# Second layer's attention in a two-layer kernel: three programs made one, and a quarter of its row maxima taken by way of ScalarE

## What is computed

```python
ct   = h @ [Wd_q | Wd_kv] + bias                 # 64 + 64 columns
q    = ct_q @ Wu_q + rope(ct_q @ Wq_r)           # 16 heads x 8
k    = ct_kv @ Wu_k + rope(h @ Wk_r)
v    = ct_kv @ Wu_v + bu_v
att  = softmax(q k^T / 12)                       # per batch and head, 1024 x 1024, no mask
x    = x + gate * ((att @ v) @ Wo + Wo_b)
```

## Time and profile before

| | us |
|---|---|
| median of three runs | 2776.39 (2762.96 to 2778.91) |
| the profiled execution | 2770.23 |
| its span | 2768.4 |
| TensorE's mean granted clock | 0.874 |
| busy: PE, DVE, ACT, POOL | 2131.2, 1554.8, 1210.0, 457.9 |

### The profile page before, as it was taken

How to read it: one execution, slowest core, us unless ns; L and a number is a source line. 1 busy time by engine, 2 the same in 40 slices (tenths; PEclk the granted TensorE clock), 3 DMA queues, 4 the chain that set the end, 5 groups by cost and what they waited for, 6 DMA issues and landing times. The chain is left out here.

```text
span 2768.4 us, 34114 instructions
## 1 busy us (share of the span) xinstructions
PE 2131.2 (77%) x11611; PEld 733.2 (26%) x11612; DVE 1554.8 (56%) x3124; ACT 1210.0 (44%) x1445; POOL 457.9 (17%) x548
## 2 busy tenths in 40 slices
PE   4346599999999999579768168888888867299964
PEld 2112133333333333323234011111111113233421
DVE  2865666665665663133433399999999923411101
ACT  2312144444444445222211047778778762155521
POOL 0000345454454542100022200000000000000000
PEclk8758599999999999689865569999999986599987
DMA  2000000000000000000011312112112010200000
GB/s 88 0 0 0 1 5 14 10 18 10 10 18 10 18 10 18 9 13 0 0 52 63 72 16 32 24 27 33 29 21 33 5 48 1 69 1 0 0 0 30
DMA packets 65751, 56.01 MB, mean 20 GB/s; under 512 B 37010, under 2 KB 49379, under 8 KB 65460
## 3 DMA queue, kind: packets, MB, share of 16 engines
q1 hardware_dynamic: 61188, 51.66, 8.3%
q10 hardware_dynamic: 4128, 2.43, 0.3%
q0 software_dynamic: 288, 0.00, 0.0%
HBM read 39.51 MB, written 13.89 MB: 19 GB/s over the span
## 5 line engine op out<-in xcount | busy, mean ns | idle before, releaser
L1370 DVE TENSOR_REDUCE h_m_half<-h_ps_max 128x1 f32<-128x512 f32 x1024 | 635.0, 684 | 35.3 <-PE h_ps_max L1277 31.2
L1353 ACT ACTIVATE h_P<-h_ps_st 128x1024 f32<-128x1024 f32 x512 | 495.2, 1022 | 110.4 <-PE h_ps_st L1296 109.6
L800 ACT ACTIVATE l_P<-l_ps_st 128x1024 f32<-128x1024 f32 (+3 forms) x384 | 307.0, 810 | 336.9 <-PE l_ps_st L707 335.5
L1277 PE MATMUL h_ps_max<-h_K,h_Q 48*128 48x512 bf16 x1024 | 209.0, 405 | 161.6 <-DVE h_m_half L1370 117.6
L707 PE MATMUL l_ps_st<-l_Q,l_K 64*128 64x512 f32 (+3 forms) x1536 | 329.1, 509 | 0.0
L884 DVE CUSTOM_DVE_ANT_0 l_masked<-l_ps_t,l_mask 128x384 bf16<-128x384 f32 (+3 forms) x512 | 230.3, 488 | 111.1 <-PE l_ps_t L665 110.6
L1306 PE MATMUL h_ps_o<-h_P,h_V 128*9 128x512 f32 x2048 | 268.9, 597 | 0.9 <-ACT h_P L1353 0.5
L887 DVE TENSOR_REDUCE l_m_half<-l_ps_t 128x1 f32<-128x512 f32 x256 | 164.9, 686 | 104.5 <-PE l_ps_t L665 102.6
L1695 PE MATMUL f_ps_h<-hT,f_W 128*128 x264 | 133.0, 651 | 74.5 <-issue 74.5
L1744 DVE TENSOR_TENSOR f_part<-f_biased,f_ps_w 128x512 f32<-128x512 f32 x33 | 22.7, 688 | 298.1 <-ACT f_biased L1722 298.1
L1277 PEld LDWEIGHTS h_ps_max<-h_K,h_Q 48*128 48x128 bf16 x1024 | 49.8, 93 | 494.5 <-DVE h_m_half L1370 437.4
(11 more groups left out here) (239 smaller groups left out, 2489.1 us busy)
## 6 DMA issues: line engine op xcount, KB each, us to landing
l_inv<-inverse_sums SPq DMA_DIRECT2D x64, 128.0 KB, 2.7
h_Q<-q_parts SPq DMA_DIRECT2D x192, 32.0 KB
h_K<-k_parts SPq DMA_DIRECT2D x192, 32.0 KB
f_W<-in_W SPq DMA_DIRECT2D x16, 256.0 KB
q_parts<-p_parts SPq DMA_DIRECT2D x4, 768.0 KB, 3.5
k_parts<-p_parts SPq DMA_DIRECT2D x4, 768.0 KB, 3.7
v_rows<-p_v_staged SPq DMA_DIRECT2D x4, 576.0 KB, 4.9
h_V<-v_rows SPq DMA_DIRECT2D x16, 144.0 KB
```

Of the source, the lines that this page charges most:

```text
L800: act.activation(P[e % PR][:, :, 0:w], ps_st[item(n, i, p) % 2][:, :, 0:w], ACT.Exp, scale=0.125).then_inc(consumed, 1)
L1277: pe.matmul(ps_max[:, (t + a) % NB, :], Q[n % NBUF][rows, p, qt * 128:(qt + 1) * 128], K[n % NBUF][rows, p, lo:lo + CH], start=True, stop= ...
L1353: act.activation(P[e % PR][:, :, :], ps_st[item(n, i, p) % 2][:, :, :], ACT.Exp, scale=1.0 / 12.0)\
L1370: dve.tensor_reduce(m_half[:, half, 2 * p + a, qt:qt + 1], ps_max[:, t % NB, :], AX.X, ALU.max, negate=True)\
```

## The change

Everything named here is the second layer's attention. Its three programs become one, `head_attention`. Its weights are loaded by 15 DMAs on ACT's queue in a small program of their own, `head_weights`, ahead of the first layer's experts. The eight products of batch 0 stand at the head of the program; those of batches 1 to 3 are put into the score loop by the table `AT`, one behind the last pair of a step, as are the output projections of batches 0 to 2. Each takes one of the two `ps_st` slots and an ACT instruction that empties it. Turning and splitting is a function `mix`, run by DVE for batch 0 and by POOL for the others. V stays on the chip. Outputs are kept in seven tiles `o`; SP sends the sums through DRAM, DVE inverts them (`invert`), POOL scales (`norm`) and adds (`join`). Loading a group takes 12 DMAs. The last group's chain of sums, scaling and projection stands at the end.

Of the 32 pairs of a group the eight in `FOLDED` (u = 4, 5, 12, 13, 20, 21, 28, 29) are no longer reduced from PSUM. ACT copies their four tiles to bf16 in `copied`, and DVE folds these by halves, 1024 to 512 to 256 elements wide, with three maxima of two operands and a last reduce, `LATER` = 5 pairs behind. So per group 64 reduces become 48, with 16 copies and four folds of four instructions.

PE's order in the score loop of group 0, first before (steps 2 and 3) and then after (the same steps). `h_ps_max` is a pair of maxima, `h_ps_st` scores or a product, `h_ps_o` values.

```diff
...
-def merge_heads(nc, S, A, l):
...
-def project_heads(nc, S, A):
...
-def head_scores(nc, S, A):
...
+def head_weights(nc, ctx, S, A):
+    def sb(name, shape):
+        return ctx.enter_context(nc.sbuf_tensor("h_" + name, shape, F32))
+    W = S.head = State()
+    W.Wd, W.bd, W.Wu, W.Wk, W.Wkv = sb("Wd", [D, 2, 64]), sb("bd", [128, 1]), sb("Wu", [64, 3, D]), sb("Wk", [D, 2, D]), sb("Wkv", [128, 2, D])
+    W.Wo, W.bv, W.cos, W.sin = sb("Wo", [128, NG, D]), sb("bv", [128, NG]), sb("cos", [128, T]), sb("sin", [128, T])
+    W.loaded = semaphore(nc, ctx, "h_weights_loaded")
+    W.count = 15
+    with nc.Block() as block:
         @block.scalar
         def _(act):
...
+            for to, x in ((W.Wd[:, 0, :], "Wd_q"), (W.Wd[:, 1, :], "Wd_kv"), (W.bd[0:64, :], "bd_q"), (W.bd[64:128, :], "bd_kv"),
+                          (W.Wu[:, 0, :], "Wq_r1"), (W.Wu[:, 1, :], "Wq_r1s"), (W.Wu[:, 2, :], "Wu_q"), (W.Wk[:, 0, :], "Wk_r1"),
+                          (W.Wk[:, 1, :], "Wk_r1s"), (W.Wkv[64:128, 0, :], "Wu_k"), (W.Wkv[64:128, 1, :], "Wu_v"), (W.bv[:, :], "bvG"),
+                          (W.cos[:, :], "cos1"), (W.sin[:, :], "sin1")):
+                act.dma_start(to, A[x]).then_inc(W.loaded, 16)
+            act.dma_start(W.Wo[:, :, :], A["WoG1"].rearrange("p (g d) -> p g d", g=NG)).then_inc(W.loaded, 16)
...
+    LEAD, TURN_AT, INVERT_AT = 6, 14, 8
+    NB, PR, NBUF, NOB, NLOAD, MIX = 3, 4, 4, 7, 12, 16
+    FOLDED = [u for u in range(NPAIR) if u // 4 % 2 and (u // 2) % 2 == 0]
+    LATER = 5
+    PROJECT = ("ct", "ka", "kb", "ku", "qa", "qb", "qu", "v")
+    AT = {}
+    for b in range(1, B):
+        for k, x in enumerate(PROJECT):
+            AT[(b - 1) * NG + k // 4, 2 + 3 * (k % 4)] = (x, b)
+    for b in range(B - 1):
+        for c in range(2):
+            AT[(b + 1) * NG + 2, 4 + 6 * c] = ("out", b, c)
...
+    order = [(x, 0) for x in PROJECT] + [("turn", 0)]
+    for n in range(NGR):
+        for i in range(NI):
+            if i == TURN_AT and n + 1 < NGR:
+                order.append(("turn", n + 1))
+            order += [("s", n, i, p) for p in range(2)]
+            if (n, i) in AT:
+                order.append(AT[n, i])
+    order += [("out", B - 1, c) for c in range(2)]
+    item = {x: k for k, x in enumerate(order)}
...
+        V = [sb(f"V{i}", [128, KT, H, M]) for i in range(2)]
         P = [sb(f"P{i}", [128, 2, CH]) for i in range(PR)]
...
+        o = [sb(f"o{i}", [128, T]) for i in range(NOB)]
+        inv = [sb(f"inv{i}", [128, T]) for i in range(2)]
+        flat = [sb(f"flat{i}", [128, HG * T // 128]) for i in range(2)]
+        moved = sb("moved", [D, T])
...
+        copied = [sb(f"copied{i}", [128, 2, 2, CH], BF16) for i in range(2)]
+        fold = [sb(f"fold{w}", [128, 2, w], BF16) for w in (512, 256, 128)]
...
+        def mix(eng, b, u, done, base):
+            a, t, w = a_[u], b_[u], u_[u]
+            at = base + (1 - u) * (MIX // 2)
+            eng.wait_ge(consumed, item[("qu", "ku")[u], b] + 1)
+            eng.tensor_tensor(a[:, :], a[:, :], cos[:, :], ALU.mult).then_inc(done, 1)
+            eng.tensor_tensor(t[:, :], t[:, :], sin[:, :], ALU.mult).then_inc(done, 1)
+            eng.wait_ge(done, at + 1)
+            eng.tensor_tensor(a[:, :], a[:, :], w[:, :], ALU.add).then_inc(done, 1)
+            eng.wait_ge(done, at + 3)
+            eng.tensor_tensor(a[:, :], a[:, :], t[:, :], ALU.add).then_inc(done, 1)
+            if b:
+                eng.wait_ge(parts_stored, 32 * b)
+            eng.wait_ge(done, at + 4)
+            eng.tensor_copy(parts[u][:, 0, :], a[:, :]).then_inc(done, 1)
+            eng.wait_ge(done, at + 5)
+            eng.tensor_tensor(a[:, :], a[:, :], parts[u][:, 0, :], ALU.subtract).then_inc(done, 1)
+            eng.wait_ge(done, at + 6)
+            eng.tensor_copy(parts[u][:, 1, :], a[:, :]).then_inc(done, 1)
+            eng.wait_ge(done, at + 7)
+            eng.tensor_tensor(parts[u][:, 2, :], a[:, :], parts[u][:, 1, :], ALU.subtract).then_inc(done, 1)
...
+        def load_part(eng, n, u):
+            src, to = (q1, k1)[u][n // NG], (Q, K)[u][n % NBUF]
+            for a in range(2):
+                lo, row = 64 * a, (n % NG) * 32 + 16 * a
+                rows = src[:, row:row + 16, :].rearrange("n (r p) t -> n r (p t)", p=2)
+                for count in (3, 2, 1):
+                    part = rows[0:count] if u else rows[3 - count].unsqueeze(0).broadcast_to([count, 8, 2 * T])
+                    eng.dma_start(to[lo:lo + 8 * count, :, :].rearrange("x p t -> x (p t)"), part).then_inc(loads[n % NBUF], 16)
+                    lo += 8 * count
...
+            def spread_sums(n):
+                sp.wait_ge(o_kept, 2 * n + 2)
+                sp.dma_start(sums1[n], o[n % NOB][8:128:32, :]).then_inc(sums_stored, 16)
+                sp.wait_ge(sums_stored, 16 * (n + 1))
+                if n >= 2:
+                    sp.wait_ge(inv_stored, 16 * (n - 1))
+                sp.dma_start(flat[n % 2][:, :], sums1[n].rearrange("j (x t) -> (j x) t", x=32)).then_inc(flat_loaded, 16)
+                sp.wait_ge(inverted, n + 1)
+                sp.dma_start(inv1[n].rearrange("j (x t) -> (j x) t", x=32), flat[n % 2][:, :]).then_inc(inv_stored, 16)
+                sp.wait_ge(inv_stored, 16 * (n + 1))
+                if n >= 2:
+                    sp.wait_ge(normed, 2 * (n - 1))
                 for j in range(HG):
...
+                    sp.dma_start(inv[n % 2][32 * j:32 * j + 32, :], inv1[n, j].partition_broadcast(32)).then_inc(inv_loaded, 16)
...
+            keep_parts(0, 1)
+            keep_parts(0, 0)
+            sp.wait_ge(ones_set, 2 * NBUF + 2)
+            sp.wait_ge(parts_stored, 32)
+            load_part(sp, 0, 0)
+            load(1)
             place_maxima(0)
             for n in range(NGR):
...
+                if n:
+                    spread_sums(n - 1)
+                if n % NG == 1 and n // NG + 1 < B:
+                    keep_parts(n // NG + 1, 1)
+                if n % NG == 2 and n // NG + 1 < B:
+                    keep_parts(n // NG + 1, 0)
+                if n + 2 < NGR:
+                    load(n + 2)
                 if n + 1 < NGR:
                     place_maxima(n + 1)
...
+            spread_sums(NGR - 1)
...
+            def free_slot(x):
+                if x >= 2:
+                    pe.wait_ge(consumed, x - 1)
+                return ps_st[x % 2]
...
+                elif kind == "out":
+                    pe.wait_ge(normed, 2 * NG * (b + 1))
+                    c = key[2]
+                    for g in range(NG):
+                        last = pe.matmul(to[:, 0:CH], Wo[:, g, :], o[(b * NG + g) % NOB][:, c * CH:(c + 1) * CH],
+                                         start=(g == 0), stop=(g == NG - 1))
...
-                if t + 2 > NB:
-                    pe.wait_ge(reduced, t + 2 - NB)
+                for x in (t - NB, t + 1 - NB):
+                    if x >= 0 and kept_by_copy(x):
+                        pe.wait_ge(max_copied, tiles_before(x, True) + 1)
+                    elif x >= 0:
+                        pe.wait_ge(reduced, tiles_before(x, False) + 1)
...
                             values(n if i else n - 1, (i - 1) % NI)
+                    if (n, i) in AT:
+                        product(AT[n, i])
             values(NGR - 1, NI - 1)
+            for c in range(2):
+                product(("out", B - 1, c))
...
+            def copy_maxima(n, u):
+                if n >= NGR or u not in FOLDED:
+                    return
+                k = n * len(FOLDED) // 2 + FOLDED.index(u) // 2
+                if k >= 2:
+                    act.wait_ge(folded, 4 * (k - 2) + 1)
+                for a in range(2):
+                    t = 2 * (n * NPAIR + u) + a
+                    act.wait_ge(max_ready, t + 1)
+                    act.activation(copied[k % 2][:, a, u % 2, :], ps_max[:, t % NB, :], ACT.Identity).then_inc(max_copied, 1)
...
+                    for s in (2 * i + LEAD, 2 * i + 1 + LEAD):
+                        copy_maxima(n + 1 + s // NPAIR, s % NPAIR)
...
+                    if (n, i) in AT:
+                        evict(AT[n, i])
...
+            def norm(n, c):
+                cols = slice(c * CH, (c + 1) * CH)
+                pool.wait_ge(inv_loaded, 16 * HG * (n + 1))
+                pool.wait_ge(o_kept, 2 * n + 2)
+                pool.tensor_tensor(o[n % NOB][:, cols], o[n % NOB][:, cols], inv[n % 2][:, cols], ALU.mult).then_inc(normed, 1)
+            def join(b):
+                for c in range(2):
+                    pool.wait_ge(consumed, item["out", b, c] + 1)
+                    pool.tensor_tensor(S.xT[:, batch(b, c)], S.xT[:, batch(b, c)], moved[:, c * CH:(c + 1) * CH], ALU.add)\
+                        .then_inc(joined, 1)
...
+            for n in range(NGR):
+                if n >= 2:
+                    for c in range(2):
+                        norm(n - 2, c)
+                if n % NG == 2 and n >= NG:
+                    join(n // NG - 1)
```

(35 more changed lines are left out.)

434 lines of the change are left out of this document (144 added, 290 removed).

## The result

The changed kernel takes 2963.57 us (median of four runs, 2962.64 to 2966.14), the kernel before 2770.01 on the same chip. The ratio is 1.0707, 95% interval 1.0679 to 1.0735: **193 us slower**. I forecast 2835, slower, and a range up to 2905. The direction holds, the range doesn't.

A forecast was written before the change was run, and what follows sets the result against it. VectorE's reduces were taken to bound the score loop. Weights +8.7, start -142.8, group 0 +7.2, loop +146, products +65 and end -24.7 sum to +59 on 2770.2, 2829; the median lies 6 higher, so 2835, range 2700 to 2905.

The forecast's parts named there:

- No cost: In the loop: sums through DRAM, POOL's scaling and share of `mix`, and 12 loads a group were to add nothing.
- Weights: Ahead of the attention: fifteen loads in a program of their own take 8.7 us on the path, +8.7.
- start: Layer norm's end to first maxima: only batch 0 projected ahead, 39.5 us long, -142.8, held to 6 either way.
- group 0: Group 0's maxima: PE's clock at half, a round trip per pair, four folds on top, +7.2 us.
- end: After the last group: 25.3 us to the next norm against 50.0, -24.7.
- Score loop, +146: Fifteen groups: copies and folds make eight pairs take 12.4 us, not 9.9; a group 50.6, not 40.84.
- Rival B: Score loop: PE's clock falls to 1.2 GHz, a round 14.7 us, loop +140, 2975; chance 0.12 with C and D.
- Products in the loop, +65: Score loop: 24 products waiting for `ps_st` slots cost 40 us, v products 4.5, six output projections 20.
- step 5: Score loop: a product here costs only 0.2 us because a fold covers it; without that cover 12 us more.
- Rival C: Score loop: folds run at the single rate or are held by POOL, +56, 2891; chance 0.12 with B and D.
- A: Score loop: copies slip in without making anyone wait, the loop keeps its pace, 2614 us; chance 0.24.
- D: Score loop: the fold doesn't relieve DVE at all, same price as C; chance 0.12 with B and C.

The follow-up runs named there:

- fold_only: The kernel before, its three programs kept, with only the copies and folds put into the middle one; 2992.5 us, ratio 1.0824.
- fold_one_wait: fold_only with one wait of TensorE for a pair of maxima where the same engine frees both buffers; 2979.8 us, 1.0745.
- nf_both: no_fold with one wait for a pair of maxima and POOL's `mix` held back until VectorE's split; 2712.6 us, 0.9783.
- nf_delay: no_fold with POOL's `mix` held back until VectorE has split the next group's maxima; 2730.0 us, 0.9841.
- pool_tiny: The changed kernel with POOL's `mix` of batches 1 to 3 on one column of 1024; 2912.9 us, 1.0527.
- no_fold: The changed kernel with `FOLDED` empty: one program, every maximum reduced by VectorE from PSUM; 2771.0 us, 0.9995.
- nf_one_wait: no_fold with one wait of TensorE for a pair of maxima in place of two; 2749.8 us, 0.9923.

## Why the prediction was wrong, and where it was right

The range failed in the score loop, where 211 were forecast and 329 measured. Four steps failed there: the clock left at its higher level (32 to 62 us by fold_only), POOL's share of `mix` under "No cost" (41 without folds, 22 to 36 with them), the products and outputs (87 for 65), and a second wait that no term had (13 to 21). They overlap in part, so they don't add up to the 118.

- *Weights, start, group 0, end.* +11.7 for +8.7, -134.9 for -142.8, +8.2 for +7.2, -24.4 for -24.7. The start missed the 6 that I gave it either way. `mix` of batch 0 was done after 27.8, as forecast; the issues of the loads took 4.4 for 2, and from the last of them to the first matmul it was 11.5 for 5.8. SP issues group 1's twelve loads in that time, but no run shows whether they are the cause. The rest of the program took 4.1 more; in the runs with one program and whole values it stays at 454 to 455, and in fold_one_wait, with three programs, it is 453.4. I have no cause for it.
- *Score loop, +146.* The step held in its mechanism. With a single wait, as the chain had it, the round at a clock of 1.00 is 12.42 for 12.4; the second wait makes it 12.59. The fold takes 1.85, and the idles lie where named. Two things failed. The four rounds of a group come to 52.8 at their best and not 50.6: about 1 is the second waits, and the rest lies at the group's end, for which I had 1.1. And the sum has TensorE's clock at its higher level throughout; "PE's clock at 1.00" stands among the signs. Rival B was given as a case of its own at 1.2 GHz throughout, while "A part of it is likelier than the whole" stood beside it and went into no number. In fold_only that part is between 32 and 62 us. The Trainium skill's section that rival B quotes ("TensorE: Matmul & The Clock Gate", "A second HAM failure mode: psum-queue depth-cycling") pointed the right way: the same round reads 1.00, 0.87 or 0.76 here.
- *Two waits for one* are in the diff, and no term had them: 21 us without folds, 13 with them.
- *Products in the loop, +65.* It was 87 by nf_both. The products are 62 of it for 44.5. With step 5 uncovered, for which the text named 12 more, it would have been 56.5, and in nf_delay, where the groups with products read 1.00 (but for group 0, as before), they cost 56 over plain ones. So the 2.0 to 2.3 a product was right, and the cover was not there without folds. Outputs are 4.0 each for 3.4.
- *"No cost".* This is the step that was wrong in kind. I priced POOL's share of `mix` at nothing, by POOL's own idle time, and asked what of it would be late, not whom it holds up. It can hold VectorE's operations that read two operands from SBUF and its casts, and the five small ones end each group on the path: 41 us in the kernel without folds, part of it clock. With them it is 22 by pool_tiny, or 36 if only the groups with products count. Rival C had named POOL, with L1145's 1.76 as its row, but for the folds alone.
- *The sum.* Fold_only's 211 are hand-overs, clock and its second waits; no_fold's 144 are 87 of products and outputs, 21 of waits and 37 to 42 of `mix`. Of the total of 355, 26 overlap. How these 26 divide between clock and hidden waits stays open. In the changed kernel 83 of the 118 that the loop missed by are in groups where products, `mix` and the clock act together, and no run parts them there.
- *The rivals.* A, that copies slip in between, is refuted: with every mend known the plain group still takes 47.0. C's single rate is refuted by the fold's 0.68. So is D: VectorE is busy for 38.2 us in a group of fold_only and for 40.4 in one of the kernel before, so the relief is there; it is the hand-over that outweighs it.

## What to carry to other kernels

Work put on an engine that stands idle isn't free until you have asked whom it holds up; let it run where the bound engine reads PSUM, and not beside the few short operations that close a stage. Before a share of the bound engine's work is given to another through the same few banks, count the hand-over: here a round of eight pairs became 2.7 us longer although VectorE was relieved of 0.6. And take a change of two halves apart first: the half worth having showed only when the other and two small side effects, a second wait and a place in time, were gone.

## What the runs showed of the hardware

- VectorE's operations with two SBUF operands, and its casts, can wait for POOL's: beside `mix` a cast of 0.18 became up to 2.25 us, a two-operand operation of 0.19 up to 1.99 and one of 0.68 up to 2.90, while reduces from PSUM kept 0.69 and their pace beside 20.6 us of POOL's work. The Trainium skill ("SBUF — State Buffer", "SBUF: two separate sides") calls the shared port pair "an exclusive lock, not a bandwidth split", and the trace agrees: the lengthened small operations of after end within 0.05 us of POOL's (lines above).
- Beside POOL's memsets of 1.80 us, which read nothing, VectorE's two-operand operations of 128x1024 in `mix` of batch 0 kept 1.22; the one cast there took 1.14, where the later ones take 0.69 (trace of after).
- A second wait on a semaphore delayed a pair of matmuls by 0.04 us (no_fold against nf_one_wait).
- A tensor_tensor of bf16 in SBUF runs at 0.68 us for 1024 outputs from 2 x 1024 inputs (1.22 for f32).
- In fold_only TensorE's granted clock changes between rounds with the same instructions: 1.00, 0.87 or 0.76, and the round takes 12.6, 13.0 to 13.1 or 13.9 to 14.4. In nf_both's plain groups it reads 1.00 throughout.
